# Layer-norm rows of the two 8-dim attentions: scaled and shifted by ScalarE instead of VectorE, on one Trainium2 core

## The reference

```python
def _layernorm(x, axis=-1, eps=1e-05):
    m = jnp.mean(x, axis=axis, keepdims=True)
    v = jnp.var(x, axis=axis, keepdims=True)
    return (x - m) / jnp.sqrt(v + eps)

x = x + tanh(g_xattn[0]) * _L0_xattn_ref(_layernorm(x), ctx_768, ...)   # 16 heads of 8 dims
x = x + tanh(g_ffn[0])   * _L0_ffn_ref(_layernorm(x), ...)              # 8 experts, two per token, gelu
x = x + tanh(g_xattn[1]) * _L1_xattn_ref(_layernorm(x), ctx_768, ...)   # 16 heads of 64 dims
x = x + tanh(g_ffn[1])   * _L1_ffn_ref(_layernorm(x), ...)              # all 8 experts, weighted
x = x + tanh(g_xattn[2]) * _L2_xattn_ref(_layernorm(x), ctx_768, ...)   # one head of 128 dims
x = x + tanh(g_ffn[2])   * _L2_ffn_ref(_layernorm(x), ...)              # 8 experts, one per token, silu
x = x + tanh(g_xattn[3]) * _L3_xattn_ref(_layernorm(x), ctx_768, ...)   # 16 heads of 8 dims again
x = x + tanh(g_ffn[3])   * _L3_ffn_ref(_layernorm(x), ...)              # ternary weights, gelu, layer norm
```

## Time and profile before

| | |
|---|---|
| median of 3 timed runs | 1072.79 us (1065.82 to 1073.53) |
| the profiled execution | 1081.44 us, span of the trace 1079.6 us |
| PE busy | 789.9 us (73%) |
| PEld busy | 676.1 us (63%) |
| DVE busy | 527.0 us (49%) |
| ACT busy | 361.7 us (34%) |
| POOL busy | 279.1 us (26%) |
| granted TensorE clock, mean | 0.817 of full speed |
| first 8-dim attention | about 10 to 139 us of the span |
| second 8-dim attention | about 862 to 1011 us of the span |

### The profile page before, as it was taken

One profiled execution on the slowest core, in us unless ns is written; L12 is line 12 of the kernel. 1 busy time (PEld: TensorE's weight loads), 2 busy tenths in 40 slices (PEclk: granted clock), 3 DMA queues, 4 the chain that ended last, 5 costly groups with the idle time before them and its releaser, 6 DMA issues.

```text
span 1079.6 us, 17933 instructions
## 1 busy us (share of the span) xinstructions
PE 789.9 (73%) x6901; PEld 676.1 (63%) x6901; DVE 527.0 (49%) x1636; ACT 361.7 (34%) x842; POOL 279.1 (26%) x229
## 2 busy tenths in 40 slices
PE   4888941876398199999998656975685755988875
PEld 3677730766388178787886445753675744777665
DVE  5576442341033466666664877433332444766421
ACT  3444400323054065555462001111332532443430
POOL 5233116523503421212121000003025052322121
PEclk9999955787789599999998776555787957988985
DMA  7424323655676200000000000002547833210000
GB/s 185 117 68 129 108 68 120 184 169 151 200 240 184 74 1 2 1 1 1 1 1 1 1 0 1 1 7 90 162 145 213 241 82 99 68 50 1 2 20 19
DMA packets 70337, 86.65 MB, mean 80 GB/s; under 512 B 8124, under 2 KB 41805, under 8 KB 70253
## 3 DMA queue, kind: packets, MB, share of 16 engines
q1 hardware_dynamic: 67181, 79.22, 25.2%
q0 software_dynamic: 3072, 6.30, 2.0%
HBM read 64.59 MB, written 20.91 MB: 79 GB/s over the span
## 4 chain that ended last, share of the span: by engine, by line
PE 55%; DVE 19%; issue 8%; DMA 5%; POOL 4%; ACT 4%; another core or an unknown queue 2%; SPq 2%; POOLq 0%; DVEq 0%; ACTq 0%
PE banks L1218 7%; PE banks L1230 5%; PE banks L928 4%; PE banks L1302 3%; PE banks L1056 3%; DVE xn L1535 3%; PE banks L929 3%; PE banks L930 3%; PE banks L970 3%; PE banks L1311 3%; DVE x L2025 3%; PE banks L1322 3%; PE banks L1068 3%; PE banks L1079 2%; PE banks L1034 2%
## 5 line engine op out<-in xcount | busy, mean ns | idle before, releaser
L810 ACT ACTIVATE hT<-banks,wdown 128x128 f32<-128x128 f32 x304 | 85.8, 372 | 160.3 <-PE banks L1218 97.3
L1218 PE MATMUL banks<-xTs,wup 128*128 128x128 f32 x608 | 94.8, 308 | 23.9 <-ACT hT L810 17.9
L1218 PEld LDWEIGHTS banks<-xTs,wup 128*128 128x128 f32 x608 | 87.5, 222 | 28.2 <-issue 28.2
L540 POOL TENSOR_TENSOR kbd<-k,const 96x1248 fp32r<-96x1248 f32 x32 | 72.4, 2268 | 103.9 <-PE banks L1056 101.7
L749 ACT ACTIVATE pT<-banks 77x512 f32<-77x512 f32 x128 | 69.4, 591 | 81.8 <-PE banks L1056 81.8
L523 POOL TENSOR_TENSOR rstd<-vv,const 128x4 f32<-128x4 f32 x24 | 24.4, 1015 | 249.3 <-DVE vv L1526 249.3
L1230 PE MATMUL banks<-wdown,hT 128*128 128x128 f32 x608 | 86.3, 291 | 0.0
L1230 PEld LDWEIGHTS banks<-wdown,hT 128*128 128x128 f32 x608 | 81.0, 208 | 0.2 <-issue 0.2
L558 POOL TENSOR_TENSOR sh<-sh,rd 128x616 f32<-128x616 f32 x32 | 38.9, 1217 | 147.1 <-DVE rd L1570 147.1
L598 POOL DMA_INDIRECT xs<-xn,slot x48 | 46.6, 971 | 101.1 <-DVE slot L1808 87.7
L1877 DVE COPY ysb<-banks 128x128 f32<-128x128 f32 x76 | 22.0, 290 | 104.0 <-PE banks L1230 88.9
(11 more groups left out here) (315 smaller groups left out, 1829.5 us busy)
## 6 DMA issues: line engine op xcount, KB each, us to landing
wdown<-in_down SPq DMA_DIRECT2D x76, 258.0 KB
wup<-in_up SPq DMA_DIRECT2D x76, 256.0 KB
q<-queries SPq DMA_DIRECT2D x24, 256.0 KB
queries<-qc SPq DMA_DIRECT2D x8, 512.0 KB, 2.7
ys<-ysb SPq DMA_DIRECT2D x16, 256.0 KB
k<-keys SPq DMA_DIRECT2D x24, 156.0 KB, 4.4
xs<-zt SPq DMA_DIRECT2D x2, 1472.0 KB, 11.8
keys<-kc SPq DMA_DIRECT2D x8, 312.0 KB
```

Source lines behind the costliest of these rows:

```text
L540: pool.tensor_tensor(kbd[b % NB8][0:96, :, :, :].bitcast(F32R), kb, m, ALU.mult).then_inc(h8.kbd, 1)
L810: ins = act.activation(hT[T % 3][:, c, :], ps[:, T % 2, c * P:c * P + P], func, bias=wdown[T % NW][:, HID + c:HID + c + 1])
L1218: ins = pe.matmul(ps[:, T % 2, c * P:c * P + P], w_[:, c * P:c * P + P], xTs[T % 3][:, :], start=True, stop=True)
```

## The change

For n in `ON_ACT`, that is 0 to 3 and 24 to 28, `front_b` on DVE no longer makes `xn`. It makes `mb` = -mean * rstd, one `scalar_tensor_tensor` of 128x4 whose two inputs `mv` and `rstd` both lie in SBUF. ACT makes `xn` = rstd * x + mb, four `activation` instructions of 128x128 with a per-row bias and a per-row scale (`scaled`). They stand at fixed places of ACT's program: n = 0 before the first `front`, n = 1 before `pick_rows(0)`, n = 24 inside the second expert block before the last tile's `hidden`, n = 25 before the second 8-dim attention, and the others between the two halves of `exps` of a batch with b % 4 == 3. A semaphore `fr.shift` tells ACT that `mb` is there; POOL and DVE wait for the `xn` before, so that `rstd` and `mb` aren't overwritten too early. To make room for the semaphore, two weight loads now count on `ld.l1raw`.

```diff
@@ -139,6 +139,7 @@
         rstd = place("rstd", [P, GB])
         fs = place("fs", [P, 5, GB])
         mh = place("mh", [P, 2, GB])
+        mb = place("mb", [P, GB])
         idn = const[:, C_ID:C_ID + P]
         xs = [a[f"xs{i}"] for i in range(4)]
         ys = [a[f"ys{i}"] for i in range(4)]
@@ -260,9 +261,9 @@
         assert s[1] <= nc.sbuf_usable_end, (s[1], nc.sbuf_usable_end)
 
 
-        ld = sems("loaded", "const", "x", "xrest", "ctx", "gate", "a", "r", "l1raw", "l1", "b", "l3")
+        ld = sems("loaded", "const", "x", "xrest", "ctx", "gate", "a", "r", "l1raw", "b", "l3")
         su = sems("setup", "zero", "rows", "hi", "lo", "tanh", "pe", "scratch", "plink", "vlink", "blank")
-        fr = sems("front", "var", "rstd", "xn", "xt", "hi", "lo")
+        fr = sems("front", "var", "rstd", "shift", "xn", "xt", "hi", "lo")
         h8 = sems("heads8", "w", "pads", "kst", "qst", "kmm", "khi", "klo", "kin", "kbd", "qmm", "qhi", "qlo", "qin", "vmm", "v",
                   "s", "max", "nt", "nq", "st", "exp", "o", "oT", "y", "x")
         mo = sems("experts", "zero", "w_mm", "w_ss", "w_rt", "w", "var", "rstd", "nn", "rn", "xn", "turn", "xT", "r",
@@ -300,6 +301,12 @@
         wup_in = (mo.wup0, mo.wup1, mo.wup2, mo.wup3)
         wdown_in = (mo.wdown0, mo.wdown1, mo.wdown2, mo.wdown3)
         back_in = (mo.gat0, mo.gat1)
+
+        ON_ACT = (*range(0, NG), *range(6 * NG, 7 * NG + 1))
+
+        def shifts(n):
+
+            return sum(m in ON_ACT for m in range(n + 1))
 
         def upto(n):
 
@@ -485,8 +492,8 @@
                          a["L1_ffn_expert_w"].rearrange("e d h -> d e h")).then_inc(ld.l1raw, 16)
             experts(0)
             wait_done(sp, "ff", 1)
-            sp.dma_start(wo1[:, :, :], a["L1_xattn_Wo"].rearrange("(c p) d -> p c d", p=P)).then_inc(ld.l1, 16)
-            sp.dma_start(bo[:, :], row(a["L1_xattn_bo"])).then_inc(ld.l1, 16)
+            sp.dma_start(wo1[:, :, :], a["L1_xattn_Wo"].rearrange("(c p) d -> p c d", p=P)).then_inc(ld.l1raw, 16)
+            sp.dma_start(bo[:, :], row(a["L1_xattn_bo"])).then_inc(ld.l1raw, 16)
 
             sp.dma_start(b_raw[:, :], a["b"]).then_inc(ld.b, 16)
             load_heads8(1)
@@ -520,6 +527,8 @@
                 if n in DROPPED:
                     return
                 pool.wait_ge(fr.var, upto(n))
+                if n - 1 in ON_ACT:
+                    pool.wait_ge(fr.xn, upto(n - 1))
                 pool.tensor_tensor(rstd[:, :], vv[:, :], const[:, C_HALF:C_HALF + GB], ALU.pow).then_inc(fr.rstd, 1)
 
             def split_chunk(src, rows, hi, lo, links, done_, count):
@@ -667,6 +676,14 @@
             def copy(o_, i_, **kw):
                 return act.activation(o_, i_, ACT.Copy, **kw)
 
+            def scaled(gn, n):
+
+                act.wait_ge(fr.shift, shifts(n))
+                for t in range(GB):
+                    ins = act.activation(xn[:, t, :], x[:, gn * GB + t, :], ACT.Identity, bias=mb[:, t:t + 1],
+                                         scale=rstd[:, t:t + 1])
+                ins.then_inc(fr.xn, 1)
+
             def front(n):
                 if n in DROPPED:
                     return
@@ -761,6 +778,7 @@
                 if run == 0:
                     for g in range(1, NG):
                         context(g)
+                    scaled(1, 1)
                     pick_rows(0)
                 own_values(0, 0)
                 for g in range(2 if run else 1, NG):
@@ -773,6 +791,8 @@
                 for b in range(B):
                     g = b // GB
                     exps(b, (0, 1))
+                    if b % GB == 3 and g < NG - 1 and NG * phase + g + 2 in ON_ACT:
+                        scaled((g + 2) % NG, NG * phase + g + 2)
                     if b % GB == 0 and g < NG - 1:
                         query_hi(g + 1)
                     exps(b, (2, 3))
@@ -822,11 +842,15 @@
                             key_hi(1, i - 4)
                         if hh == 3 and i == 8:
                             pick_rows(1)
+                        if hh == 3 and i == 13:
+                            scaled(0, 6 * NG)
                         if h == 0 and i == 3:
                             turned(hh + 1)
                         if h == 0 and i == 8:
                             tanh(hh + 1)
                 front((2 + 4 * run) * NG)
+                if run:
+                    scaled(1, 6 * NG + 1)
 
             def heads64():
                 def prepare(g):
@@ -910,6 +934,7 @@
                      ps[0:DC, 3 + g, 0:GB * SP].rearrange("p (b t) -> p b t", b=GB)[:, :, 0:SK]).then_inc(su.hi, 1)
 
             context(0)
+            scaled(0, 0)
             front(0)
             heads8(0, 0)
             experts(0, ACT.Gelu)
@@ -1316,7 +1341,7 @@
                             ins.then_inc(h64.o, 1)
 
                 def project(g, b):
-                    pe.wait_ge(ld.l1, 32)
+                    pe.wait_ge(ld.l1raw, 96)
                     pe.wait_ge(h64.oT, 2 * (4 * g + b) + 2)
                     for c in range(C1):
                         pe.matmul(ps[:, 6, 0:P], oT[:, c, :], wo1[:, c, :], start=(c == 0), stop=False)
@@ -1531,6 +1556,12 @@
                 if n in DROPPED:
                     return
                 dve.wait_ge(fr.rstd, upto(n))
+                if n in ON_ACT:
+                    if n - 1 in ON_ACT:
+                        dve.wait_ge(fr.xn, upto(n - 1))
+                    dve.scalar_tensor_tensor(out=mb[:, :], in0=mv[:, :, 0], scalar=-1.0, in1=rstd[:, :], op0=ALU.mult,
+                                             op1=ALU.mult).then_inc(fr.shift, 1)
+                    return
                 for t in range(GB):
                     ins = dve.tensor_scalar(xn[:, t, :], x[:, bass.ds(gn * GB + t, 1), :].rearrange("p o d -> p (o d)"),
                                             mv[:, t, 0:1], rstd[:, t:t + 1], ALU.subtract, ALU.mult)
```

## The result

The changed kernel took 1055.15 us (median of 4 runs, 1053.24 to 1055.96), the kernel before on the same chip 1069.94 us (4 runs, 1065.82 to 1073.53). The ratio is 0.986, with a 95% interval of 0.9814 to 0.9907. That is a gain of 14.8 us, with 10.0 to 19.9 in the interval. Medians are over all executions of a kernel, while ratios, and the means further down, leave out the executions that lie more than 1.5% above its fastest.

The account below looks back on a forecast made before the run. PE was taken to stand 2.70 to 2.99 us for `nm` in batches where POOL's `kbd` holds DVE's `xn`. The terms -11.1 - 8.6 + 5.2 + 5.8 + 1.0 = -7.7 took 1072.8 to 1065.1 us, range 1057 to 1075.

Parts of the forecast that it names:

- The waits that end: In four batches with a `front_b`, PE's waits of 2.70 to 2.99 us for `nm` end: -11.1 us.
- The clock in the batch behind: Behind those four waits PE keeps full clock and each next batch takes 6.40 us: -8.6 us, bounds 0 and 8.6.
- the late exponentials: In four batches ACT's `xn` delay the second exponentials and row `q`, PE losing 1.1 or 1.5 us each: +5.2 us.
- `mb` is held: In the batches DVE's `mb` ends only when POOL's `kbd` does, at 54.8 instead of 53.4 in the first.
- rival 1: `mb` is not held by `kbd`, saving the 5.2 and 1.0 us: -13.9 us, 1058.9 us; chance 0.20.
- ACT's four `xn`: Per moved front, four scalings on ACT take 0.46 us each, 0.35 apart: 1.5 us.
- The start: Before the first scores, `pick_rows` stands behind the scaling of n = 1: +5.8 us, bounds 1.4 and 5.8.
- The junction: Between experts and second attention, scalings of n = 24 and 25 come later on ACT: +1.0 us, bounds 0 and 1.5.
- The sum: Over the whole kernel the terms give -7.7 us, applied to the timed median of 1072.8: 1065.1 us.
- rival 2: In the batches the clock falls although PE waits only 1.1 to 1.5 us: +0.9 us, 1073.7 us; chance 0.15.
- rival 3: At the start the delay is covered by a late DMA of the queries: -13.5 us, 1059.3 us; chance 0.08.
- rival 4: ACT's two-pointer scalings cost twice or more, say 3.6 us for four: +17.7 us, 1090.5 us; chance 0.05.

Follow-up runs that it names:

- ends: The change with only n = 0, 1, 24 and 25 scaled on ScalarE, the other fronts on VectorE; 1092.09 us, ratio 1.0046 to the kernel before.
- final: The change with only n = 2, 3, 26, 27, 28 on ScalarE, and POOL's `kbd` waiting for `mb` except at n = 27; 1052.84 us, ratio 0.9857.
- both: The change with only n = 2, 3, 26, 27, 28 on ScalarE, and POOL's `kbd` waiting for `mb`; 1067.51 us, ratio 0.9796 to the kernel before.
- late_one: The change with the call `scaled(1, 1)` moved from before `pick_rows` to behind the copies of the second group's keys; 1075.21 us, ratio 0.9858.
- polite_27: The kernel before with POOL's `kbd` waiting for VectorE's `xn` at n = 2, 3, 26, 28, not 27; 1047.62 us, ratio 0.9841.
- batches: The change with only n = 2, 3, 26, 27, 28 scaled on ScalarE, the other four fronts on VectorE; 1076.48 us, ratio 0.9893 to the kernel before.

## Why the prediction was right or wrong

**The waits that end (-11.1).** Right. The batches with a `front_b` went from 8.61 to 5.85 us twice in the first run, from 9.70 to 6.90 and from 8.62 to 5.85 in the second: 2.76, 2.76, 2.80 and 2.77, together 11.1.

**The clock in the batch behind (-8.6) and the late exponentials (+5.2).** The mechanisms are right. In the first run the clock falls to half behind each of the two waits in all four profiles that have these waits (before three times, and "ends"), and at neither place in the eleven others; at 58.96:66.41 it is full. With `mb` free the same batch takes 6.28 us, where I had booked 6.40; with `mb` held it takes 7.45, so the hold costs 1.17 us against 1.1. For the two batches of the first run the net was forecast as -0.6 and came out as -0.7. In the second run the batch behind n = 27 went from 8.79 to 7.89 us, as forecast (-0.9). The one behind n = 28 went from 9.81 to 6.73, 3.1 us instead of 1.9. Here I had read a row wrongly: I took 6.40 us for this batch from "a batch of the same content", but batch 12 of the second run has no queries of a next group to make (`queries(g + 1)` is called in the first three groups only). Free, it takes 5.59 us, as "final" shows:

```profile
978.55:988.35 9.80, 9.80 (x93) 8.13 (x93) 3.65 (x6) 3.41 (x6) 1.71 (x1) 0.50 0.01 2
```

```profile
944.31:949.90 5.59, 5.59 (x97) 4.60 (x93) 3.80 (x6) 3.40 (x7) 2.90 (x2) 1.00 0.01 3
```

So 4.2 us of clock fell due there and not 3.4, and the hold cost 1.1 and not 1.5. The third profile of before has 8.67 us for this batch: the size of the term depends on how long the clock stays at half, and that varies (the granted clock over this batch is 0.50 in the shown trace and 0.61 in the third).

**`mb` is held.** Right, against rival 1: 1.54 us beside `kbd`, 0.15 to 0.17 without. The rule that I had cited from the Trainium skill (SBUF — State Buffer, "Who interferes with whom"), that the later of a two-input VectorE instruction and a GpSimd instruction waits for the whole of the other, agrees with this trace: `mb` took 1.54 us and ended 0.02 us behind `kbd`. So it does with `wl` in "both", two inputs as well, which took 2.65 us and ended 0.55 us behind the second key matrix (943.08 against 942.53).

**ACT's four `xn` (1.5 us).** Measured 1.65 us, 0.48 each with starts 0.39 apart. That is 0.15 us in each place, and it decided nothing. Here the Trainium skill had the nearer price (ScalarE: Activation LUTs, "What ACT_TABLE_LOAD costs"): 186 ns and 0.833 ns per element, with about 93 ns for each pointer operand, give an estimate of 479 ns for 128 columns and two pointers, and the median of the 36 is 479.

**The start (+5.8).** Right in mechanism and nearly in size: 37.13, 37.75, 37.58 and 37.09 us against 32.22, 31.67 and 31.80, in the mean +5.5. The run with the moved call, at 32.55 us, confirmed that `pick_rows` behind the waiting scaling was the path. In the shown trace it is 4.9: the first scores (the old L1034) began at 33.51 where I had 34.4.

**The junction (+1.0).** Mis-sized, within its bounds: 25.06, 25.86, 25.63, 26.80 against 25.38, 25.55, 25.42 is +0.4. ACT waited 3.41 us for `mb` of n = 24 and the last gelus ran behind it, and the junction grew by 0.4 us only; what covered the rest I have not traced.

**The sum.** The stages that the change touches, with batch 1 of the first run (4.92 to 7.13 us over all profiles, as the clock rises in it or before it: in "before, shown" the transpose at its start takes 0.47 us and the one at its end 0.33) and batch 3 of the second, which waits for a DMA, left out, are in the mean of all profiles +5.5 (start), -6.3 (first run), +0.4 (junction) and -8.7 us (second run): -9.1, where I had -7.7. The time fell by 14.8 us in the first comparison. So no term is off by more than some 1.2 us. The clock term of 8.6 us was, if anything, too small: with the free batches of the runs (6.28 us twice, 5.59 us) in place of 6.40, and 2.4 us kept for the batch behind n = 27, which no run shows free, it is 2 x 1.53 + 4.2 + 2.4 = 9.7 us.

The step that failed is the last one, 1072.8 - 7.7 = 1065.1 us. It took the median of three runs and the whole rest of the program as fixed and put nothing in the sum or in the range for either. Of the 10.0 us between 1065.1 and 1055.15, the runs show this:

- 2.9 us are the median of before, which came out at 1069.94 with a fourth run and not at 1072.79. With the old median the same gain would have given 1058.0 us, inside the range.
- 1.4 us are the terms above: in the means over the profiles 0.6 are the junction, 0.4 the batches and 0.3 the start.
- 5.7 us stand in no stage that the change touches.

Is it a clock that is higher elsewhere? In the profiles it is not. In the two 8-dim runs, from batch 2 of the first on, TensorE was at half clock for 47.4, 47.0 and 36.7 us before and for 14.0, 19.1, 26.2 and 14.7 after, worked out from the granted clock of each run. That is 25 us less in the mean, 21.6 of them at the four waits and behind them, and it raises the mean clock of the whole execution by 0.012. The timed executions rose by 0.010 and 0.015 (next table). Over the rest of the program the mean clock is 0.790 to 0.800 before and 0.790 to 0.801 after. Within a sitting the time falls by 0.71 to 0.85 us for each 0.001 of mean clock, so by this estimate the 21.6 us, which are 0.010 of mean clock, are worth 7 to 8.5 us, near the 8.6 that I had booked.

The next table has the means of the timed runs (change is after2 and after3 of the record, late_one the moved call, kbd_waits the change with POOL waiting for `mb`, polite the kernel before with POOL waiting for `xn`, final and polite_27 the two without the wait at n = 27), the difference to before, and beside it what the stages of the traces add up to, again against the mean of the three profiles of before and without the two varying batches:

| sitting | kernel | time, us | mean clock | against before | by the stages |
|---|---|---|---|---|---|
| second | before | 1083.6 | 0.8154 | | |
| second | change | 1072.9 | 0.8250 | -10.7 | -9.1 |
| second | batches | 1075.2 | 0.8192 | -8.4 | -13.8 |
| second | ends | 1089.2 | 0.8176 | +5.6 | +4.6 |
| third | before | 1084.2 | 0.8155 | | |
| third | late_one | 1072.4 | 0.8240 | -11.8 | -15.4 |
| third | kbd_waits | 1078.8 | 0.8190 | -5.4 | -6.3 |
| third | polite | 1073.2 | 0.8185 | -11.0 | -9.5 |
| third | both | 1067.7 | 0.8238 | -16.5 | -10.8 |
| fourth | before | 1067.4 | 0.8167 | | |
| fourth | change | 1054.3 | 0.8314 | -13.1 | -9.1 |
| fourth | final | 1051.8 | 0.8230 | -15.6 | -17.1 |
| fourth | polite_27 | 1049.9 | 0.8257 | -17.5 | -12.3 |

The stages give the timed difference of each kernel within 6 us, on either side, and the 5.7 us of the first comparison are no more than that. With 3 to 10 runs of a kernel, and one trace of most, a difference of this size can't be told from scatter. But it need not be scatter: the gain was 14.8 and 13.1 us in the two sittings in which the changed kernel's first expert FFN was short, and 10.7 and 10.4 (one execution of each kernel) in the two in which it was long, and no execution of before with the short stage was profiled. So the cause of these 5.7 us stays open.

**The range.** Its lower end came from rivals 1 and 3 alone. But the kernel before, unchanged, spreads over 8 to 21 us within a sitting (all executions), a spread of 7.7 us was known and used for the chances alone, and the profiles of one kernel differ by up to 11 us in the last FFN. Rival 1 was refuted by the 1.54 us of `mb`, rival 2 (the clock falls all the same) by the full clock behind it, rival 3 (the start is covered) by the first L1045 at 37.13 us, and rival 4 by 1.65 us for four. That the direction was right rests on the terms; that the time missed the range by 2 us, and not more or not at all, is chance. The opening has one weak reading: 96 instructions at 1.12 us for four are 26.9 us when nothing disturbs them, not far from the 32 us of the chain, so it was the waits of PE that pointed to `xn`, and not its share.

## What to carry to other kernels

When an instruction is long because another engine holds it, first try to move the holder: one wait on POOL did here what moving the work to ScalarE did (ratios of 0.986 both). Then look what stands on the held engine at the holder's new time, since a key matrix that was 0.94 us late met the next two-input instructions and cost 6.7 us in two batches. A call that is put ahead of ready work in an in-order queue costs its own wait in the stage behind it, so place it where its input is due. Before a batch is used as the measure of another, count what each has to do; and a range must hold the scatter of the median and of the stages that the change doesn't touch.

## What the hardware showed that I had not expected

- A `tensor_tensor` of 128x512 with two inputs from SBUF (`wl`) took 2.65 us beside POOL's key matrix and 0.69 alone, and the two key matrices beside `wpr` and `wl` took 4.95 us together instead of 4.51: in a row of such instructions each engine waits for the other in turn, and both lose.
- One copy of ScalarE with both scale and bias per row took 0.48 us for 128 columns (0.48 to 0.49 over all 36), and four of them 1.65 us.
- The mean granted clock of the kernel before, unchanged, went from 0.799 to 0.827 within one sitting, and over the executions of a sitting the time was shorter by 0.71 to 0.85 us for each 0.001.
- The first expert FFN has two lengths, 174 to 179 and 195 to 200 us, with the same instructions and 205 to 214 against 180 GB/s from its 50th us on. In each of the four sittings of the experiments all profiles had the same one; what sets it is not known.
